# Weight splitting ahead of a projection, an attention's end in halves, and repeated products on TensorE

## What is computed

```python
def attention(xn, ctx):                       # 16 heads of 16, 1601 context rows
    q, k, v = heads(xn @ Wq), heads(ctx @ Wk), heads(ctx @ Wv)
    return merge(softmax(q @ k.T / 4) @ v) @ Wo

x = x + attention_0(layernorm(x), ctx)
u = layernorm(x)                              # mixture: 2 shared and 8 routed experts, 2 of 8 per token
x = x + u + shared_experts(u) + top2_experts(u)
x = x + attention_1(layernorm(x), ctx)
n = layernorm(x)
real = n @ cos(theta + theta_noise)
imag = n @ sin(phi + phi_noise)
x = x + sqrt(real * real + imag * imag)
```

## Time and profile before

| what | value |
|---|---|
| median of 3 runs | 1283.85 us (1282.34 to 1285.02) |
| the profiled execution | 1282.03 us |
| its span, first to last instruction | 1280.3 us |
| mean granted TensorE clock | 0.987 |
| PE / DVE / ACT / POOL busy | 1169.2 / 727.2 / 1015.8 / 172.4 us |
| exponentials of the first attention | from 51.25 us on, 400 of them |
| exponentials of the second attention | from 866.95 us on, 400 of them |

### The profile page before, as it was taken

The page is one execution under the profiler, slowest core; times in us unless marked ns, Lnnn a source line. Parts: engine busy times, 40 slices in busy tenths (PEclk is TensorE's granted clock), DMA queues, the critical chain, the costliest instruction groups (busy, mean ns, idle before and its releaser), DMA issues. The chain is left out here.

```text
span 1280.3 us, 43524 instructions
## 1 busy us (share of the span) xinstructions
PE 1169.2 (91%) x17822; PEld 584.3 (46%) x17822; DVE 727.2 (57%) x1694; ACT 1015.8 (79%) x1482; POOL 172.4 (13%) x205
## 2 busy tenths in 40 slices
PE   8888898898897999999999999988889999999894
PEld 5422232232232356767899998752223323322232
DVE  5325767757756577554566666662546445434346
ACT  3599998998999946363466666639999999999992
POOL 5111111011001030233000011032321000000000
PEclk9999999999999999999999999999999999999997
DMA  6236734633635425131344445133110010010001
GB/s 193 66 114 206 254 119 129 204 101 122 221 116 176 155 62 166 38 111 46 116 119 116 118 136 160 49 98 94 50 55 23 19 29 3 19 29 2 2 3 66
DMA packets 106305, 124.94 MB, mean 98 GB/s; under 512 B 25091, under 2 KB 89310, under 8 KB 106142
## 3 DMA queue, kind: packets, MB, share of 16 engines
q1 hardware_dynamic: 89088, 85.95, 22.0%
q0 software_dynamic: 9328, 29.37, 7.4%
q10 hardware_dynamic: 7726, 7.26, 1.9%
HBM read 70.27 MB, written 46.95 MB: 92 GB/s over the span
## 5 line engine op out<-in xcount | busy, mean ns | idle before, releaser
L914 ACT ACTIVATE prob<-banks 128x1024 f32<-128x1024 f32 x800 | 748.8, 1060 | 18.6 <-PE banks L1766 14.9
L1801 PE MATMUL banks<-prob,v 64*32 64x512 f32 x6400 | 437.9, 595 | 0.0
L1766 PE MATMUL banks<-zone,kst 52*32 52x512 f16 x6144 | 316.9, 384 | 65.4 <-ACT prob L914 57.9
L1766 PEld LDWEIGHTS banks<-zone,kst 52*32 52x32 f16 x6144 | 86.9, 89 | 445.2 <-ACT prob L914 427.5
L1801 PEld LDWEIGHTS banks<-prob,v 64*32 64x32 f32 x6400 | 117.6, 106 | 25.0 <-issue 3.1
L2437 PE MATMUL banks<-xsT_d,w 128*128 128x128 f16 x1776 | 123.6, 219 | 2.4 <-DMA w<-weight_parts 1.1
L2437 PEld LDWEIGHTS banks<-xsT_d,w 128*128 128x128 f16 x1776 | 108.6, 98 | 11.3 <-issue 8.4
L2448 PE MATMUL banks<-w,hh 128*128 128x256 f16 x592 | 107.0, 273 | 0.0
L2234 DVE TENSOR_TENSOR hl<-hid,hh 128x128 f16<-128x128 f32 x296 | 83.1, 291 | 30.5 <-ACT hh L2161 22.7
L2157 ACT ACTIVATE hid<-banks,b 128x128 f32<-128x128 f32 x222 | 74.5, 369 | 25.0 <-PE banks L2437 21.2
L2400 PE MATMUL banks<-w,hh 128*128 128x256 f16 x480 | 80.6, 276 | 2.1 <-DVE outb_d L2319 2.1
(11 more groups left out here) (291 smaller groups left out, 1378.6 us busy)
## 6 DMA issues: line engine op xcount, KB each, us to landing
weight_parts<-late SPq DMA_DIRECT2D x54, 256.0 KB, 3.3
w<-weight_parts POOLq DMA_DIRECT2D x24, 512.0 KB, 3.9
late<-in_L_ffn_W_r SPq DMA_DIRECT2D x43, 256.0 KB, 4.1
weight_parts<-more SPq DMA_DIRECT2D x26, 256.0 KB, 3.6
zone<-q_parts SPq DMA_DIRECT2D x180, 32.0 KB
slot_rows<-late POOLq DMA_DIRECT2D x14, 384.0 KB, 4.4
more<-in_L_ffn_W_r SPq DMA_DIRECT2D x21, 256.0 KB, 4.1
xs_d<-slot_rows ACTq DMA_DIRECT2D x39, 128.0 KB, 2.1
```

The lines of the kernel that those rows point to most:

```text
L914: nc.scalar.activation(prob[:, t % P_RING, 2 * (n % 2):2 * (n % 2) + 2, :], score[G % S_RING], ACT.Exp, scale=0.25).then_inc(exp_done, 1)
L1766: last = nc.tensor.matmul(score[G % S_RING][j:j + GROUP, a, :], kst[stack, 2 * q + n % 2, t * P + j:t * P + j + GROUP], qst[stack, u % Q_R ...
L1801: last = nc.tensor.matmul(outp[u % 2][GROUP * j:GROUP * (j + 1), a, :], v[rows, t, u % NQ, j, :], prob[rows, (u * KT + t) % P_RING, j if t ...
```

## The change

It has three parts.

1. In layer 0, in the second unit of each chunk (q = 1), VectorE's order changes. Where there is a previous chunk (chunks 1 to 3), all pieces of weights of this unit come ahead of `add_projection`; in chunk 0 the pieces behind the first come behind `take_last`. SyncE waits for one more semaphore ahead of the load of the first expert's weights.
2. The end of layer 1 is done per half of 256 tokens: moments, root (now on ScalarE), reciprocal, normalisation, turns, high and low part for each half, and the waves of the first half before the turns of the second.
3. In that end TensorE repeats a product of the feed-forward weights with themselves, into a bank that is overwritten later: 12 times behind the last unit, 4 and 8 times behind the two halves' projections, 4 times behind the first turns.

```diff
@@ sync, u == UNITS - 2
                     sp.wait_ge(scores_done, PAIRS * (UNITS - 2))
+                    sp.wait_ge(side_done, at["last", NC - 1, NQ - 3] + 1)
@@ gpsimd
-            scales(NC - 1)
             if first:
+                scales(NC - 1)
@@ scalar, end of layer 1
-                for h in range(DH):
-                    act.wait_ge(side_done, at["xturn", c, h] + 1)
-                    nc.scalar.activation(xpT[:, 0, h, :], side_bank("xturn", c, h), ACT.Copy).then_inc(tail_high, 1)
+                for h in range(2):
+                    act.wait_ge(ovar_ready, c + h + 1)
+                    nc.scalar.activation(orstd[:, 2 * h:2 * h + 2], ovar[:, 2 * h:2 * h + 2], ACT.Sqrt).then_inc(tail_root, 1)
+                    act.wait_ge(tail_turned, h + 1)
+                    nc.scalar.activation(xpT[:, 0, :, h * D:(h + 1) * D], turn_bank(h).rearrange("p (d s) -> p d s", d=DH),
+                                         ACT.Copy).then_inc(tail_high, 1)
                 for i in range(TPC):
-                    act.wait_ge(side_done, at["wave", c, i] + 1)
+                    act.wait_ge(tail_waved, i + 1)
@@ vector, layer 0
                 if first and q == 1:
-                    cuts(u, 0, 1)
+                    cuts(u, 0, CUTS if done else 1)
                     if done:
                         add_projection(c - 1, 1)
                         out_moments(c - 1)
                     if ahead:
                         untangle(c + 1, 0)
-                        cuts(u, 1, 2)
                         untangle(c + 1, 1)
-                    else:
-                        cuts(u, 1, 2)
                     take_last(u)
                     if done:
                         out_normalise(c - 1)
-                    cuts(u, 2, CUTS)
+                    else:
+                        cuts(u, 1, CUTS)
@@ vector, last_waves
                     if i:
                         final_tile(i - 1)
+                    else:
+                        final(NC - 2)
@@ vector, end of layer 1
+            def last_normalise(h):
+                dve.wait_ge(tail_root, h + 1)
+                nc.vector.reciprocal(oscale[:, 2 * h:2 * h + 2], orstd[:, 2 * h:2 * h + 2]).then_inc(tail_scale, 1)
+                dve.wait_ge(tail_scale, h + 1)
+                for i in (2 * h, 2 * h + 1):
+                    nc.vector.tensor_scalar(on[:, i, :], g.x[:, (NC - 1) * TPC + i, :], omv[:, i, 0:1], oscale[:, i:i + 1],
+                                            ALU.subtract, ALU.mult).then_inc(tail_normed, 1)
                 finish_halves()
                 add_projection(c, 0)
+                last_moments(0)
+                last_normalise(0)
+                add_projection(c, 1)
+                take_last_turned(0)
+                last_moments(1)
+                last_normalise(1)
                 final(0)
-                add_projection(c, 1)
-                out_moments(c)
+                take_last_turned(1)
                 final(1)
-                out_normalise(c)
-                for h in range(DH):
-                    take_last_turned(h)
-                final(2)
                 last_waves()
@@ tensor, end of layer 1
+            def keep_running(count):
+
+                for n in range(count):
+                    nc.tensor.matmul(wave_bank(0), g.wave[:, 0, 0, 0:P], g.wave[:, 0, 0, :], start=True, stop=True)
+
+            if not first:
+                pe.wait_ge(side_free, sides_before(UNITS))
+                keep_running(12)
+                for i in range(DH):
+                    for n in range(2):
+                        for k in range(DH):
+                            project_out(c, i, n, k)
+                    keep_running((4, 8)[i])
+                last_turns(0)
+                keep_running(4)
+                pe.wait_ge(tail_low, 1)
+                last_wave(0)
+                last_turns(1)
+                last_wave(1)
+                pe.wait_ge(tail_low, 2)
+                last_wave(2)
+                last_wave(3)
+                return
```

More of the change, by code:

```diff
@@ L305, in attention @@
             tail_step, tail_high, squared = (sem(n) for n in ("tail_step", "tail_high", "squared"))
+            tail_root, tail_scale, tail_normed, tail_turned, tail_low, tail_waved = (
+                sem(n) for n in ("tail_root", "tail_scale", "tail_normed", "tail_turned", "tail_low", "tail_waved"))
         m_added, m_stat, m_var, m_rstd, m_xn, m_turned, m_copied, m_query, m_split, m_qstored = (
@@ L360, in side_bank, with turn_bank, wave_bank @@
             return outp[(u + 1) % 2][:, at[name, c, i] % 2, :] if u < UNITS else tailbank[at[name, c, i] % len(tailbank)]
+        def turn_bank(h):
+            return tailbank[(at["out", NC - 1, 0] + DH + h) % len(tailbank)]
+        def wave_bank(i):
+            return banks[:, 2 * S_RING + i, :]
         def packed(c, i):
@@ L936, in _ @@
                     root(n * TPC, (n + 1) * TPC)
[L937 to L939 removed]
+                for h in range(2):
[4 more added lines that the diff above has]
+                                         ACT.Copy).then_inc(tail_high, 1)
                 for i in range(TPC):
[L941 removed]
+                    act.wait_ge(tail_waved, i + 1)
                     if i >= 2:
                         act.wait_ge(power_ready, c * TPC + i - 1)
[L944 removed]
+                    nc.scalar.activation(square[i % 2], wave_bank(i), ACT.Square).then_inc(squared, 1)
                     if i:
@@ L1512, in final_tile, with last_moments @@
                 nc.vector.tensor_tensor(g.x[:, n, :], g.x[:, n, :], power[:, n, :], ALU.add).then_inc(final_done, 1)
+            def last_moments(h):
+                base = 2 * TPC * (NC - 1) + 4 * h
+                for n in range(2):
+                    dve.wait_ge(ostat_step, base + n + 1)
+                    nc.vector.bn_aggr(omv[:, 2 * h + n, :], ostats[:, 2 * h + n, :]).then_inc(ostat_step, 1)
+                dve.wait_ge(ostat_step, base + 4)
+                nc.vector.tensor_scalar_add(ovar[:, 2 * h:2 * h + 2], omv[:, 2 * h:2 * h + 2, 1], LN_EPS).then_inc(ovar_ready, 1)
+            def last_normalise(h):
[5 more added lines that the diff above has]
+                                            ALU.subtract, ALU.mult).then_inc(tail_normed, 1)
             def take_last_turned(h):
+                tokens = slice(h * D, (h + 1) * D)
                 dve.wait_ge(tail_high, h + 1)
-                nc.vector.tensor_tensor(xpT[:, 1, h, :], side_bank("xturn", NC - 1, h), xpT[:, 0, h, :], ALU.subtract).then_inc(side_free, 1)
+                nc.vector.tensor_tensor(xpT[:, 1, :, tokens], turn_bank(h).rearrange("p (d s) -> p d s", d=DH),
+                                        xpT[:, 0, :, tokens], ALU.subtract).then_inc(tail_low, 1)
             c = NC - 1
@@ L1955, in output_ahead, with last_turns, last_wave @@
                                          start=(h == 0 and k == 0), stop=(h == HT - 1 and k == 2))
+            def last_turns(h):
+                pe.wait_ge(tail_normed, 2 * (h + 1))
+                for d in range(DH):
+                    for i in range(2):
+                        last = nc.tensor.transpose(turn_bank(h)[:, (2 * d + i) * P:(2 * d + i + 1) * P],
+                                                   on[:, 2 * h + i, d * P:(d + 1) * P], g.ident[:])
+                last.then_inc(tail_turned, 1)
+            def last_wave(i):
+                for h in range(DH):
+                    for k, (a, b) in enumerate(PRODUCTS):
+                        last = nc.tensor.matmul(wave_bank(i), xpT[:, b, h, i * P:(i + 1) * P], g.wave[:, a, h, :],
+                                                start=(h == 0 and k == 0), stop=(h == DH - 1 and k == len(PRODUCTS) - 1))
+                last.then_inc(tail_waved, 1)
+            def keep_running(count):
+                for n in range(count):
+                    nc.tensor.matmul(wave_bank(0), g.wave[:, 0, 0, 0:P], g.wave[:, 0, 0, :], start=True, stop=True)
             c = NC - 1
             hidden_ahead(0, 6)
+            if not first:
+                pe.wait_ge(side_free, sides_before(UNITS))
+                keep_running(12)
+                for i in range(DH):
+                    for n in range(2):
+                        for k in range(DH):
[11 more added lines that the diff above has]
+                return
             for i in range(DH):
@@ L1967, in _ @@
             hidden_ahead(12, 15)
[L1968 to L1976, removed]
+            logits(c)
+            hidden_ahead(15, EARLY * HT)
+            for i in range(AHEAD):
+                output_ahead(i)
 def experts(nc, g):
```

## The result

The changed kernel takes 1263.12 us, the median of four runs (1261.12 to 1264.51), beside 1283.09 us before in the same comparison (1281.87 to 1285.02): the ratio is 0.9838 (0.982 to 0.9857), 20.0 us less. I had predicted 1266.2 us and a range of 1263.2 to 1271.5. The direction and both mechanisms hold. The time lies 0.08 us under the range, and the sum had no term for a part of what was gained.

What follows compares the result with a forecast made beforehand. ScalarE's exponentials (748.8 us) were taken as the bound, with gaps in the first attention and an exposed end. 11.0 + 6.6 = 17.6 us off the 1283.85 us median gave 1266.2 us, range 1263.2 to 1271.5.

Steps and rivals of the forecast that it cites:

- Part 1: First attention, third units of chunks 1 to 3: earlier pieces remove ScalarE's gaps, 11.0 us gained; 8.3 to 11.3.
- the fourth piece's load: Layer 0, ahead of the projection: load issued at 177.21, taken as 5 us, between no wait and 7.8 us.
- My price for a gap: First attention: ScalarE's gap is one and a half times TensorE's wait, 0.6 us a place for 0.4 us.
- Part 2: End of layer 1 in halves of 256 tokens: last VectorE instruction at 1271.5 instead of 1278.13, 6.6 us gained.
- four sums and four tile ends, 8 x 0.43: Last VectorE work of the end, without a pause: eight instructions at 0.43 us each, finishing at 1271.5.
- The step that failed: Whole kernel: gains of 11.0 and 6.6 us summed to 17.6 us, with no term for other stretches.
- best case for the two parts: First attention and end together: at most 11.3 and 7.5 us gained, used for the range's low end.
- Rival 2: First attention: stall shrinks, late load or GpSimd's port leaves 1 to 1.5 us a place; 1270.2 us, chance 0.12.
- Rival 3: End: TensorE cold or the repeated products in the way, only 3 us gained there; 1269.9 us, chance 0.13.
- Rival 4: First attention: part 1 does nothing, something else holds the same product; 1277.2 us, chance 0.02.
- Rival 5: Layer 0: fourth piece holds VectorE once its load takes 9.8 us, kernel slower; 1287.9 us at 17 us, chance 0.01.
- the low end of my bounds: End of layer 1: TensorE's clock at its lower level, waves and repeats slower, 3 us gained.

Runs made afterwards that it cites:

- experiment 1: Kernel before the change with part 1 alone (order of the pieces, SyncE's wait) and the old end: 1270.95 us, ratio 0.9901.
- experiment 3: Kernel before the change, only GpSimd's split of the rows moved behind VectorE's finish of that unit, pieces left in place: 1272.07 us, ratio 0.991.
- experiment 6: Changed kernel with 5 instead of 8 repeated products in front of the first turns: 1263.29 us, ratio 0.9836, end 24.78 us.
- experiment 4: Changed kernel without its repeated products, one run: 1263.18 us, end 25.15 us.
- experiment 5: Kernel before the change plus part 1, old end kept, with repeated products in that end's pauses, one run: 1268.59 us, end 29.14 us.
- experiment 8: Changed kernel itself, unaltered, timed and profiled again in another comparison: 1263.39 us, ratio 0.9836, end 25.34 us.
- experiment 2: Changed kernel with VectorE's old order of pieces in layer 0 (parts 2 and 3 alone, SyncE's added wait kept): 1277.42 us, ratio 0.9952.
- experiment 7: Changed kernel without any repeated product, timed and profiled a second time: 1262.83 us, ratio 0.9839, end 26.92 us.
- experiment 9: Changed kernel with 16 instead of 8 repeated products in front of the first turns, one run: 1264.85 us, end 27.06 us.
- experiment 10: Changed kernel with 5 instead of 8 repeats before the first turns and nine more in layer 1's preparation: 1261.13 us, ratio 0.9823.

## Why the prediction came out as it did

**Part 1, 11.0 us predicted, 11.5 measured at its three places.** The mechanism is as told, step by step: four pieces between 174 and 181, `take_last` unmoved, `finish` at 193.40 for 194.5 (1.05 us of it because everything at this place is earlier), its two lines at 0.75 and 0.69 us beside GpSimd, the sum 2.0 us ahead of TensorE's need. The one step whose unknown I took from another place, the fourth piece's load, was at most 3.75 us where I took 5. In the next two chunks VectorE waited 2.65 and 1.74 us for it. The units fell by 4.41, 4.19 and 2.92 us, 11.52 together, where I had 11.33 of idle rows less 0.1 us a place. In the first two the idle rows (4.42 and 4.19) were the whole loss, so nothing was to be taken off; in unit 14 they (2.72) were 0.2 short. The rest of the 11.73 lies in units that vary between profiles by as much (unit 3 in experiment 1). My price for a gap, one and a half times TensorE's wait, holds only with a low spell: 2.89 us of pause cost 2.92 without one. The 4.2 us of gap that I took off the four units from 203.72 to 301.18 should be 3.7 (0.65 and 3.08), which makes a unit 23.4 us; nothing hangs on it.

The contention was the cause of most of what I had called lateness. I read 2.36 us at 196.30 as one price among several; experiment 3 shows that it, with the 1.40 us ahead of it, was 2.5 of the 2.88 us. That GpSimd's split would not hold `finish` was right: its instructions ran in 1.04 and 2.15 us beside lines 1238 and 1241. The rule of the Trainium skill (SBUF — State Buffer, Who interferes with whom), that VectorE contends with GpSimd in a two-port mode or with two inputs from SBUF, agrees with both places: lines reading PSUM beside GpSimd took their usual 0.75 and 0.69 us, and the line with two SBUF inputs in experiment 3 was held for 2.15 us.

**Part 2, 6.6 us predicted, 7.25 measured.** Counted from the last exponential's end, `finish_halves` ended at 8.48 us in both kernels. The first normalised half was ready at 11.49 us (predicted 11.74), ScalarE's copy ended at 13.40 (13.45), the low part at 14.11 (14.14), the second half's low part at 17.75 (17.94), `final(1)` at 18.89 (19.14). Up to there the working is good to 0.3 us. Its last term, "four sums and four tile ends, 8 x 0.43", was mis-sized: 3.44 us predicted, 2.97 measured (1252.89 to 1257.00, less `final(2)`). It put a duration where a distance belongs: the instruction takes 0.43 us when it stands alone at the end, but back to back these start every 0.33 to 0.34 us (the chain above). With `final` at 1.13 instead of 1.2 the last VectorE instruction ended at 22.99 us instead of 23.84. Two things run against it: the store behind it took 2.35 us instead of 2.13, and ScalarE's copy began 0.56 us later than with five repeats (experiment 6), which I had set at 0.4.

**The step that failed** is the one that put everything outside the two parts at nothing: "11.0 + 6.6 = 17.6 us", taken off the median before. In the two profiles 20.9 us were gained, 3.3 more. Of these, 0.5 are part 1's idle rows and 0.65 the end, mostly the 8 x 0.43. The largest share, 2.0 us (0.85 and 1.14), lies ahead of and between the attentions, where the change moves no work. These stretches go with the low spells of the clock, which lie differently in every profile. Ahead, the kernels with a spell at 10 us (before, and experiments 3, 4 and 5) take 51.25 to 51.76 us, and all others 49.98 to 50.78. Between, the unaltered change took 428.26 in its first profile and 430.62 in experiment 8, and before lies within that with 429.40. So the 1.14 us between are less than the 2.36 by which two profiles of one kernel differ, and the 0.85 ahead come and go with the spell at 10 us; that the clock is the whole cause of both is argued from this, not shown.

The range failed by the same step. Its best case for the two parts, 11.3 + 7.5 = 18.8 us, was met (11.5 + 7.25), but the medians gained 20.0 us here, and 21.8 in the comparison of experiment 8 (1285.18 less 1263.39). The 1.8 us for the runs' spread nearly took this up, counted from 1283.85 where this comparison has 1283.09, and the low end missed by 0.08 us. One candidate for the gain beyond 18.8 is the third stall: its pause brought no low spell in the profile of before, but in experiment 2 it did and cost 1.3 us more. No run tells how often that is so.

**The rivals.** Rival 2 fell: no gap stayed at any of the places, and the load was in time. Rival 3 was half right: the repeats do stand in the way, by 0.56 us, but TensorE was not at its lower level; in experiment 7, where it was for two spells, the end still gained 5.7 us where I had set 3. Rival 4 fell with experiment 1. Rival 5 needed a load of 9.8 us and met 3.75. On my sentence about the Trainium skill (TensorE: Matmul & The Clock Gate, part 1), that the moment of the change differs from run to run: the spells of one and the same kernel did lie elsewhere in each profile (from the last attention product to the last wave none in either profile of the change; without repeats, one in experiment 4 and two in experiment 7), but no profile's end fell to the low end of my bounds.

## What to carry to other kernels

Before moving work out of the way of a late instruction, look whether one of the instructions in front of it is longer than its like elsewhere; here moving GpSimd's instruction out of its way brought nearly the same 11 us as reordering the work. Take the cost of a run of instructions from start to start in a place where they are back to back, and the cost of a stall from the length of the whole unit against an undisturbed one. Compare stretches that the change does not touch in two profiles of one kernel before putting their difference at nothing. Repeated products that keep TensorE's clock up pay by their place: put them where its pause is on the path and end them before its next operand is there, and do not expect them to show in a median where the work behind them has slack, as here.

## What the runs showed of the hardware

- A pause of TensorE can cost more than its length where a backlog stands behind it: 2.88 us of waiting and 3.40 us at 1.2 GHz made 4.42 us for ScalarE. A pause of 2.89 us cost 2.92 us without the low spell (unit 14 before) and 4.25 with it (unit 14 in experiment 2).
- VectorE's scalar_tensor_tensor of 512 columns with two SBUF inputs took 2.15 us beside GpSimd's tensor_tensor and 0.75 alone; its tensor_scalar from float32 to float16 took 2.36 us beside it and 0.48 alone. GpSimd's instruction took 2.47 us in the stall of before, but 2.15 both beside lines that read PSUM and in experiment 3, where it held line 1232.
- Repeated products of 512 columns cost 0.216 us each at 2.4 GHz, to the last one (experiment 9).
- The same rows of TensorE's work in layer 1's preparation (line 1682's last four products and line 1686's eight) took 1.80 and 1.97 us where the clock fell 0.4 us behind their start (experiment 8), and 1.13 and 1.08 us where it fell later, behind the same pause of 2.35 us (the change's first profile), or not at all (experiment 10).
